# A cross-attention and FP4 feed-forward kernel: prologue, first batch and end reordered, transposes of the maxima moved, one VectorE instruction per pair of maxima

## The reference

```python
def block(x, ctx):                        # per batch
    q = heads(layernorm(x) @ Wq.T + bq);  k = heads(ctx @ Wk.T + bk);  v = heads(ctx @ Wv.T + bv)
    att = softmax(q @ k.T / 4) @ v        # 16 heads
    x = x + merge(att) @ Wo.T + bo
    n = layernorm(x)
    gate = fp4(n) @ fp4(w_gate).T;  up = fp4(n) @ fp4(w_up).T
    return x + fp4(silu(gate) * up) @ fp4(w_down).T

def fp4(x):                               # blocks of 16 along the last axis
    scale = max(max(abs(block)) / 6, 1e-12)
    return nearest_of_grid(x / scale) * scale     # 0, .5, 1, 1.5, 2, 3, 4, 6 with sign
```

## Time and profile before

| | us |
|---|---|
| median of 3 runs (lowest, highest) | 1885.5 (1876.26, 1885.63) |
| the profiled execution, its own time | 1876.45 |
| its span, first to last instruction | 1874.7 |
| TensorE busy | 1702.6 (91%) |
| VectorE busy | 1367.7 (73%) |
| ScalarE busy | 1154.8 (62%) |
| GpSimd busy | 521.7 (28%) |

### The profile page before, as it was taken

The page is one execution under the profiler, slowest core; times in us unless marked ns, Lnnn a source line. Parts: engine busy times, 40 slices in busy tenths (PEclk is TensorE's granted clock), DMA queues, the critical chain, the costliest instruction groups (busy, mean ns, idle before and its releaser), DMA issues. The chain is left out here.

```text
span 1874.7 us, 26516 instructions
## 1 busy us (share of the span) xinstructions
PE 1702.6 (91%) x9600; PEld 667.1 (36%) x9600; DVE 1367.7 (73%) x1598; ACT 1154.8 (62%) x2335; POOL 521.7 (28%) x407
## 2 busy tenths in 40 slices
PE   3669889999999999999999999999999999989857
PEld 2323213433343333433343334433343334323325
DVE  2677877678777877678878787678877787788236
ACT  2136566776667656676667656776667656666631
POOL 4215521052203422062302522062302522012202
PEclk8779899999999999999999999999999999999979
DMA  6821324232140414232150324233060323200000
GB/s 148 159 35 55 78 45 89 42 92 39 61 83 29 90 33 95 36 85 52 39 105 29 81 42 95 35 71 66 25 119 29 77 35 59 36 1 4 6 15 12
DMA packets 98030, 109.08 MB, mean 58 GB/s; under 512 B 18788, under 2 KB 83308, under 8 KB 97900
## 3 DMA queue, kind: packets, MB, share of 16 engines
q1 hardware_dynamic: 93344, 103.26, 26.6%
q10 hardware_dynamic: 4556, 4.13, 1.1%
HBM read 76.78 MB, written 30.16 MB: 57 GB/s over the span
## 5 line engine op out<-in xcount | busy, mean ns | idle before, releaser
L838 ACT ACTIVATE prob<-st 128x512 f32<-128x512 f32 (+1 forms) x1664 | 904.1, 597 | 458.4 <-PE st L649 456.8
L893 DVE TENSOR_REDUCE cmx<-mx 128x4 f32<-128x2048 f32 x352 | 806.2, 2290 | 301.5 <-PE mx L663 299.6
L649 PE MATMUL st<-qstack,kstack 112*128 112x512 bf16 (+1 forms) x1664 | 532.6, 388 | 36.7 <-ACT prob L838 23.9
L678 PE MATMUL pvb<-prob,vv 128*17 128x512 f32 (+1 forms) x3328 | 441.8, 603 | 0.0
L649 PEld LDWEIGHTS st<-qstack,kstack 112*128 112x128 bf16 (+1 forms) x1664 | 130.8, 98 | 568.0 <-issue 312.8
L663 PE MATMUL mx<-kstack,qstack 48*128 48x512 bf16 (+1 forms) x2048 | 250.5, 338 | 57.3 <-DVE cmx L893 33.4
L1163 POOL TENSOR_TENSOR ht<-ht,rh 128x704 f32<-128x704 f32 x30 | 41.6, 1387 | 464.4 <-DVE rh L1033 464.4
L605 PE MATMUL misc<-wguT,rowsT 128*128 128x352 f32 x460 | 156.4, 462 | 0.8 <-ACT rowsT L787 0.8
L1130 POOL TENSOR_TENSOR cin<-cin 128x400 f32<-128x400 f32 (+1 forms) x60 | 55.3, 922 | 350.5 <-ACT cin L769 350.5
L663 PEld LDWEIGHTS mx<-kstack,qstack 48*128 48x128 bf16 x2048 | 56.0, 94 | 214.3 <-issue 148.6
L576 PE MATMUL misc<-wv,ctxT 128*128 128x256 f32 (+1 forms) x392 | 104.1, 388 | 0.0
(11 more groups left out here) (178 smaller groups left out, 1593.1 us busy)
## 6 DMA issues: line engine op xcount, KB each, us to landing
kstack<-scr_k SPq DMA_DIRECT2D x384, 100.1 KB, 4.4
scr_k<-cin SPq DMA_DIRECT2D x48, 300.0 KB, 3.2
qstack<-scr_q SPq DMA_DIRECT2D x372, 32.0 KB, 2.4
cin<-ctx_in SPq DMA_DIRECT2D x8, 1280.0 KB, 7.8
scr_q<-qp SPq DMA_DIRECT2D x15, 384.0 KB, 2.8
scr_k<-cin SPq DMA_DIRECT2D x16, 300.8 KB, 3.3
xn<-x SPq DMA_DIRECT2D x8, 512.0 KB, 3.8
x<-x SPq DMA_DIRECT2D x8, 512.0 KB, 3.8
```

Source lines behind the costliest of these rows:

```text
L649: mm(st[0:KROWS[kt], h, :], kstack[:, hd, KOFF[kt]:KOFF[kt] + KROWS[kt]], qstack[:, hd, :], start=True, stop=True).then_inc(st_full, 1)
L678: last = mm(pvb[32 * h:32 * h + D + 1, :], vv[0:w, kt, HG * g + h, :], prob[0:w, n % 2, h, :], start=(kt == 0), stop=(kt == NKT - 1))
L838: activate(prob[0:KROWS[kt], n % 2, 2 * pair + h, :], st[0:KROWS[kt], h, :], ACT.Exp, scale=SCALE).then_inc(exp_done[2 * pair + h], 1)
L893: v.tensor_reduce(cmx[:, g % 2, h0:h0 + 2, at0:at1 + 1:at1 - at0], mx[:, :, :, :].rearrange("p j h n -> p h j n"), op=ALU.max, axis=AX.X). ...
```

## The change

In words, part by part:
- `maximum_of_two` is gone: every product has its own reduction of 128 x 1024 elements. The catch-up in "first" is three products in each of ten steps.
- The transposes of the maxima (`nm`) of groups 1 and 3 go from steps 8 and 33 to 10 and 35, `pvT` 2 from 41 to 42. The weights' jobs (`wT`, W_SCALE_AT, W_POWER_AT) come later in "first".
- Prologue: the layer norm of batch 1 is done in steps 12 to 14 of "pre" instead of in "first"; SP and ScalarE wait for group 0's queries and keys before they issue what comes next; weight loads, raw weights, the next x and the row of maxima change places; the bias product goes from step 33 to 45, with its GpSimd copies.
- "last": from step 35 on the second pair's scores go to the first half of `mx`, free by then.
- "tail": the output projection sums over the first half of the columns first; the feed-forward's input is normalised and rounded in two halves by VectorE (`half`); FP4 rounding of rows 0 to 2 on GpSimd, with magic numbers in a buffer for each row; row 3 on VectorE.
- VectorE's short one-input instructions (division by 6, the factor 1 - 2^-24, the variance's epsilon and half) become `scalar_tensor_tensor` with a second input.

The diff, cut:

```diff
-M_LATE = M_LEAD - NKT
-BIAS_AT = STEPS - M_LEAD - 1
+CATCH_UP = 2 * M_LEAD - M_GROUP
+BIAS_AT = STEPS - 7
+WIDE = 35
-PARTS = {"pre": ("early",), ...
+PARTS = {"pre": ("early", "next"), ...
@@ SLOTS
-    8: ([("ctxT", 6, "early")], [("nm", 1, "att")]),
-    9: ([("k", 0, "early")], [("xnT", 0, "early")]),
-    10: ([("k", 1, "early")], [("xnT", 1, "early")]),
-    11: ([("k", 2, "early")], [("wT", 0, "once")]),
+    8: ([("ctxT", 6, "early")], [("xnT", 0, "early")]),
+    9: ([("k", 0, "early")], [("xnT", 1, "early")]),
+    10: ([("k", 1, "early")], [("nm", 1, "att")]),
+    11: ([("k", 2, "early")], []),
...
-    33: ([("gate", 6, "late"), ("wT", 10, "once")], [("nm", 3, "att")]),
-    35: ([("down", 1, "late")], []),
+    33: ([("gate", 6, "late"), ("wT", 6, "once")], []),
+    35: ([("down", 1, "late")], [("nm", 3, "att")]),
...
+    1: ([("pvT", 3, "late")], []), 2: ([("attT", 0, "late")], [("attT", 1, "late")]), 3: ([("o", 0, "late")], []), 4: ([("o", 1, "late")], []),
+    5: ([("xqT", 0, "late")], []),
+    6: ([("gate", 0, "late"), ("gate", 1, "late")], [("up", 0, "late"), ("up", 1, "late")]),
+    7: ([("gate", 2, "late"), ("gate", 3, "late")], [("up", 2, "late"), ("up", 3, "late")]),
+    8: ([("xqT", 1, "late")], []),
...
@@ extras
+PRE_EXTRA = {
...
+    12: [("next", "stats", 0), ("next", "stats", 1)], 13: [("next", "mean", 0), ("next", "root", 0)], 14: [("next", "apply", 0), ("next", "apply", 1)],
+    1: DVE_EXTRA[1], 3: [("late", "half", 0)], 4: [("late", "half", 1)], 6: [("late", "hscale", 0)],
+    7: [("late", "hpower", 0), ("late", "hscale", 1), ("late", "hpower", 1)], 9: [("late", "hscale", 2), ("late", "hpower", 2)],
+    10: [("late", "hscale", 3), ("late", "hround", 3)],
-W_SCALE_AT = {1: 0, 4: 1, 15: 2, 18: 3, 25: 4, 28: 5}
-W_POWER_AT = {3: 0, 6: 1, 17: 2, 20: 3, 27: 4, 30: 5}
+W_SCALE_AT = {17: 0, 18: 1, 26: 2, 29: 3, 35: 4, 39: 5}
+W_POWER_AT = {19: 0, 21: 1, 28: 2, 30: 3, 37: 4, 41: 5}
+TAIL_POOL = {0: POOL_WORK[0], 6: [("late", "hscaled", 0)], 7: [("late", "hround", 0)], 8: [("late", "hround", 1)], 9: [("late", "hround", 2)]}
@@ maxima
-            if it.kind == "first" and n < M_LATE:
-                first, number = M_GROUP + 4 * n, 4
+            if it.kind == "first" and n < CATCH_UP:
+                first, number = M_GROUP + 3 * n, 3
+        def score_bank(it, n, pair, h):
+            return mx[:, 0, h, :] if it.kind == "last" and n >= WIDE and pair else st[:, h, :]
@@ prologue, SP
                 ctx_in_rows(it, "early")
+                x_in(it, "next")
                 sp.wait_ge(c_link, 4)
                 keys_out(it, 0, range(4))
                 keys_in(it, 0, "early")
+                sp.wait_ge(q_stack[0], STACK)
+                sp.wait_ge(k_stack[0], STACK)
                 sp.wait_ge(c_link, 6)
                 queries_in(it, 1, "early")
                 keys_in(it, 1, "early")
-                x_in(it, "next")
                 queries_out(it, 1)
                 keys_out(it, 1, range(4))
                 ctx_in_rows(it, "next")
+                maxima_in(it, 0, "early")
                 queries_in(it, 2, "early")
                 keys_in(it, 2, "early")
-                maxima_in(it, 0, "early")
@@ scores, TensorE
+                        if not wide or n == WIDE and pair == 0:
+                            need(pe, exp_done[2 * (1 - pair) + h], it.count("att", STEPS, n + pair))
+                        elif n > WIDE:
+                            pe.wait_ge(exp_done[2 * pair + h], it.count("att", STEPS, n))
@@ prologue, ScalarE
-                    if it.kind == "pre" and n == 5:
-                        weights_in()
                     if it.kind == "pre" and n == 14:
                         first_queries()
+                        act.wait_ge(q_stack[0], STACK)
+                        act.wait_ge(k_stack[0], STACK)
+                        weights_in()
+                    if it.kind == "pre" and n == 47:
                         raw_in(0)
                         raw_in(1)
@@ VectorE
+            def scaled(out, maxima):
+                return v.scalar_tensor_tensor(out, maxima, 1.0 / 6.0, tiny[0:out.shape[0], 0:out.shape[1]], op0=ALU.mult, op1=ALU.max)
+            def below(ap):
+                return v.scalar_tensor_tensor(ap, ap, 1.0 - 2.0 ** -24, ap, op0=ALU.mult, op1=ALU.min)
-                def maximum_of_two(first, second):
...
+                    elif what == "half":
+                        two, cols, words = slice(2 * k, 2 * k + 2), slice(32 * k, 32 * (k + 1)), slice(512 * k, 512 * (k + 1))
+                        dve.wait_ge(free["o"], c(2, k + 1))
...
+                        dve.wait_ge(full["o"], c(2, 2))
+                        for t in (2 * k, 2 * k + 1):
+                            last = v.tensor_scalar(xq3[:, t, :], x1[:, t, :], mv[:, t, 0:1], rs[:, t:t + 1], ALU.subtract, ALU.mult)
...
-                    for both in (todo[:2], todo[2:]):
-                        if both and all(job[5] < M_HEADS - 1 for job in both):
-                            maximum_of_two(*both)
-                        else:
-                            for job in both:
-                                maximum(job)
+                    for job in todo:
+                        maximum(job)
```

226 lines of the change are left out of this document (131 added, 95 removed).

## The result

The changed kernel takes **1818.0 us** (median of four runs, 1817.6 to 1818.4) against 1881.0 us (four runs, 1876.3 to 1885.6): a ratio of 0.967, 95% interval 0.963 to 0.970. The forecast was 1790, its range 1768 to 1826. The sign and the range held; 28 us of the gain that was summed up are missing. They can be found stretch by stretch: in both tables of windows the stretches are cut at the first and the last score matmul of an iteration.

A forecast was written before the change was run, and what follows sets the result against it. TensorE was taken to set the loop's pace, with stalls elsewhere. Gains of 11 (prologue), 29 (first iteration), 20 (loops), 14 (last) and 11 (tail) sum to 85, rounded to 86, from 1876.45 us: 1790 us, range 1768 to 1826.

The forecast's parts named there:

- The first ten steps: First iteration: catch-up spread to 3 products in each of 10 steps takes 45 us instead of 64.4, -19.
- Steps 10 to 51: First iteration: of 15 us of stall in 167.7, 10 are won although the weights' work moves there.
- Rival (b): Early gains halve, as weight work only moves and half clock stays: 20 us fewer, 1810; chance 0.15.
- The prologue: Before the first iteration: new order of transfers and single maxima instructions give -11 us, bounds -4 and -15.
- Loops: Six loop iterations: moving group 3's transpose removes its stall, less 0.5 us each for singles: -20, bounds -6 and -26.
- Last: Last iteration: wide banks from step 35 and the moved transpose give -14 us, bounds -7 and -18.
- Tail: After the last iteration: input quantised in halves and rounding on GpSimd give -11 us, bounds -5 and -16.
- (a): Loop iterations: VectorE late more often, singles and shifted split cost 3 us each, the 20 vanish: 1810; chance 0.17.
- (c): More gain: nearly all first-iteration stalls go and the wide banks give all: 1772 us; chance 0.15.
- (d): VectorE becomes the bound throughout, each of 45 pairs costs TensorE 0.21 us: 1876, no change; chance 0.02.
- (e): Slower: group 1's row of maxima misses its group at step 13, +34 us, 1910; chance 0.02.
- (f): The change partly misses its aim, wide banks or halves give nothing: 1801 us; chance 0.05.

The follow-up runs named there:

- experiment 1: Changed kernel with the first iteration's weight powers moved one to six steps later and the weight transposes to steps 25 to 48: 1810.5 us.
- experiment 2: Changed kernel with the weights rescheduled again, transposes mostly four or five steps behind their piece's power: 1803.3 us.
- experiment 6: Changed kernel with one instruction for two products' maxima put back wherever a step has two full ones, except the catch-up steps: 1827.0 us.
- experiment 8: Changed kernel with the loads of the first two raw weight pieces moved from the prologue to step 3 of the first iteration: 1812.1 us.
- experiment 5: Changed kernel with the maxima transpose and split of group 3 put back from step 35 to step 33: 1843.0 us.
- experiment 4: Changed kernel with the quantisation of the feed-forward input spread over one step more, its multiply moved from step 12 to 13: 1809.4 us.
- experiment 3: Changed kernel with the maxima transpose and split of group 1 moved from step 10 to step 9: 1822.9 us.
- experiment 9: Changed kernel without the separate banks for the second pair of heads in the last iteration: 1825.0 us.
- experiment 10: Changed kernel with scale and reciprocal corrections put back from two-input to one-input instructions: 1813.8 us.
- experiment 11: Changed kernel with the edits of experiment 2 (late transposes switched sides), experiment 4 and experiment 8, later GpSimd fills, SyncE's row wait, value projections singly: 1788.2 us.
- experiment 12: The kernel of experiment 11 with the scale and reciprocal corrections in one-input form as well: 1783.9 us.

## Why the prediction was right or wrong

**The first ten steps** were right: 44.4 us for a forecast of 45.

The kernel's time lay in the range because the range was wide. The first iteration's term, -10.7 us, lay outside its own bounds of -16 and -36.

**Steps 10 to 51 are the step that failed.** It read "the weights' work comes back in steps 17 to 41, spread thinner; I count 10 of the 15". The count was of total work against spare time. The profile shows +9.3 instead, and experiments 1 and 2 why: the places matter, not the total. With the places moved and GpSimd's work equal, the stretch takes 163.9 us, 3.8 below before; all of the 13 us between it and the changed kernel were order. In the old order the first two pieces had their powers at steps 3 and 6 and their transposes from 11 and 13 on, and only the four later ones stood three steps apart; two of their transposes made the long steps 20 and 23 (7.6 and 7.2 us), which lie 7.9 us above two plain steps, half of the 15 us of stall that the prediction took for spare. In the new order all six stand three or four apart. For the four wide pieces power, 6.8 us of rounding and VectorE's lag need more than three: with three the waits for GpSimd stayed (experiment 1), with four or five they were gone (experiment 2). And the power of piece 1 stands ahead of a split in the same step. The prediction priced a small instruction behind GpSimd at up to 3 us for group 1 and didn't carry that price to the other splits. Rival (b), "The early gains halve, since weight work on VectorE and GpSimd only moves and half clock stays", named this cause, and its 1810 is nearer to 1818 than the forecast. But the first ten steps' gain came in full, and the rest didn't halve but turned into a loss.

**The prologue** was -4.6 for -11. Its terms: the products' stretch was forecast at -6, and is -5.5 (37.8 against 43.3); experiment 6 gives 8 for the single form. The first product was forecast 5 us earlier (2 by the order, 3 by the transfers) and came at 45.54 instead of 47.7: ScalarE was some 2 us ahead as forecast (the input's copies at 16.65 instead of 18.98), but the cast ended with the fill, as in the kernel before, and so all of the 2 us were lost there. The 2.2 us that the first product gained lie behind the cast, where 3 were forecast. What wasn't in the sum at all is the row of maxima, 3.4 us later by the raw weights' loads (experiment 8). The prediction looked at SyncE's queue for the row, said "this gives nothing", and left out that ScalarE's 0.7 MB had moved to the same moment.

On the cast the Trainium skill, "SBUF — State Buffer", section "Who interferes with whom", has the rule that fits: copies and casts in a two-port mode exclude any GpSimd instruction, while a VectorE instruction with two SBUF inputs meets only one that reads SBUF. The trace agrees: the subtraction at 19.60, beside the same kind of fill, took its usual 0.58 us, the cast behind it 2.47. The prediction cited the other half of that rule and didn't ask which fills the casts would meet.

**Loops**: -22.1 for -20: an iteration without half clock fell by 3.1 us (2.9 forecast), which gives 18.6, and most of the other 3.5 is half clock that went with the stall (2.7 forecast). Group 3's transpose is worth what was read from the stall: 3.4 us, and 3.6 an iteration in experiment 5, half clock included. The charge for late singles was 0.5; step 14 costs 0.77, but experiment 6 shows that pairs have it too (5.00). It isn't the singles. In the kernel before VectorE still idled 0.85 us in front of the maxima of step 12; in the changed one it has no gap from step 10 to step 14, now that group 1's split stands there, and the 3.2 us of quantisation make it late. Spreading these mends it (experiment 4), moving the split by one step doesn't (experiment 3), so the split's share is argued and not shown. The 9 us more of VectorE time that the single form was charged were 2.8: back to back two singles cost 0.07 us more than a double one, not the 0.15 that was read from rows of each by itself, nor the 0.125 beside it. Experiment 3 shows how narrow the margin at group 1 is, though in VectorE's time, not in the row's: no score waited for the row.

**Last**: -11.3 for -14. Plain steps came to 1.95 where 2.1 to 2.2 was forecast. "The others 2.5" failed: steps with gate, up or down jobs gained nothing, step 45 lost 0.47. Experiment 9 puts the wide banks at 8.3 us instead of 10. The transpose gave its share (steps 33 and 34 4.6 us shorter), but steps 13 and 14 became 1.7 us longer, most of it at half clock, which was not in the sum.

**Tail**: -9.5 for -11. The first gate came 20.1 us after the first addition (forecast 19, before 23.3), and 29.3 us lie between it and the last rounding instruction's start (34.6 before). The two terms came to 3.2 and 5.3 us where 4.7 and 6.5 were forecast; 1 us more was won elsewhere, mainly ahead of the first addition.

**Other forms**: forecast 0; experiment 10 shows the held row alike in both.

Rivals (a), (c), (d), (e) and (f) didn't come true. That experiment 11 lands at 1788, near the forecast's 1790, is luck: it holds edits that the prediction knew nothing of. The two misplacements alone, the weights (14.7 us in experiment 2) and the raw loads (3.5 us in experiment 8), give an estimate of 1800.

## What to carry to other kernels

When work is moved to fill idle time, check for each moved piece not only that there is room but what stands next to it: which in-order engine will meet its result, how many steps after the start it is ready, and which short instructions will share GpSimd's time. Here the engines' totals said nothing on this; a table of step lengths by iteration, taken from one kind of matmul, shows it at a glance. And a short transfer on the critical path deserves a look at every queue that issues within some microseconds of it, not only its own.

## What the runs showed beyond the expectation

Part of what a stall costs is paid in granted clock. In steps 10 to 51 of the first iteration TensorE waited 16 us for maxima and for GpSimd, at a clock of 0.92; with 4 us of such waits left (experiment 2) the clock was 0.99. Of the 13 us between the two, 8 are TensorE's own busy time. It isn't in proportion: experiment 1 took the waits down to 10 us and the clock stayed at 0.92. And once the clock fell in one version and not in the other, with the same waits ahead of it: in experiment 11's profile it went to 0.50 at 1589.8 us, 0.3 us before step 14 of the last iteration began, and in experiment 12's it stayed at 1.00. In step 13 the two versions differ by 0.05 us of VectorE's time. The step took 5.0 us in one, 3.5 in the other, and 4.6 to 5.7 in all other versions of the changed kernel. What made the clock fall there isn't shown.

Also, three different instructions of VectorE of 0.2 to 0.3 us ended one after the other with three of GpSimd of 1.9 to 2.4 us: a chain of small linked instructions beside a chain of long ones took the pace of the long ones.
